# Neighbourhood attention with a mixture of experts: the combination's third array held in SBUF

## The reference

```python
x = x + _L0_conv_ref(_ln_c(x), ...)        # 7x7 neighbourhood attention, 16 heads, projection
t = _to_tokens(x)                          # 25088 tokens of 128 channels
t = t + _L0_ffn_ref(_ln_t(t), ...)         # experts
x = _from_tokens(t, x)

# _L0_ffn_ref: two of eight experts for each token
combine = (one_hot(topk_i, E) * topk_p[..., None]).sum(axis=1)
for e in range(E):
    h = relu(x_flat @ W1[e] + b1[e])
    out = out + combine[:, e:e + 1] * (h @ W2[e] + b2[e])
```

## Time and profile before

| | us |
|---|---|
| median of 3 runs | 3022.98 |
| lowest and highest | 3019.34, 3025.69 |
| the profiled execution | 3022.68 |
| its span, first to last instruction | 3020.9 |
| start of the second block (SP's first issue) | 2264.74 |
| first product of the experts | 2270.64 |
| last scatter issued by POOL | 2860.12 |
| first add of the combination, L1350 | 2868.77 |
| last add of the combination | 3017.23 |

### The profile page before, as it was taken

How to read it: one execution, slowest core, us unless ns; L and a number is a source line. 1 busy time by engine, 2 the same in 40 slices (tenths; PEclk the granted TensorE clock), 3 DMA queues, 4 the chain that set the end, 5 groups by cost and what they waited for, 6 DMA issues and landing times. The chain is left out here.

```text
span 3020.9 us, 112796 instructions
## 1 busy us (share of the span) xinstructions
PE 2688.8 (89%) x31346; PEld 2395.9 (79%) x31451; DVE 2269.4 (75%) x12559; ACT 2114.3 (70%) x5724; POOL 1583.9 (52%) x2025
## 2 busy tenths in 40 slices
PE   4789999999999999999999999999939999999733
PEld 2789999899989998999899989999936766776522
DVE  2668888788878887888788868888857888888655
ACT  1567878787878886887787868888847777777500
POOL 2135555455545554555455545555565777777600
PEclk9999999999999999999999999999969999999855
DMA  2665666555546664656566645566645444444399
GB/s 48 153 122 124 129 124 123 112 122 127 126 102 130 124 124 102 130 128 124 101 127 128 129 99 124 125 125 129 132 91 105 97 94 97 97 94 97 101 323 322
DMA packets 714047, 378.50 MB, mean 125 GB/s; under 512 B 422528, under 2 KB 669984, under 8 KB 713504
## 3 DMA queue, kind: packets, MB, share of 16 engines
q1 hardware_dynamic: 660704, 235.97, 40.3%
q10 hardware_dynamic: 24192, 81.67, 9.5%
q0 software_dynamic: 28608, 54.48, 6.1%
HBM read 233.43 MB, written 98.11 MB: 110 GB/s over the span
## 5 line engine op out<-in xcount | busy, mean ns | idle before, releaser
L1061 ACT ACTIVATE pr<-sc,nmx 128x100 f32<-128x100 f32 x3136 | 923.9, 369 | 61.9 <-DVE nmx L678 60.9
L962 POOL TENSOR_TENSOR oml<-om 128x256 f16<-128x256 f32 x784 | 479.6, 612 | 907.3 <-DVE om L708 890.4
L533 PE MATMUL bank<-vwin,pt 100*128 100x65 f32 x6272 | 806.2, 272 | 36.3 <-DVE om L708 28.1
L678 DVE CUSTOM_DVE_ANT_0 sc<-bank,near 128x100 f32<-128x100 f32 x3136 | 633.5, 257 | 253.7 <-PE bank L511 207.8
L533 PEld LDWEIGHTS bank<-vwin,pt 100*128 100x128 f32 x6272 | 773.4, 194 | 54.3 <-ACT pt L1069 39.5
L511 PE MATMUL bank<-kimg,held 128*128 (+2 forms) x9408 | 628.2, 216 | 40.9 <-issue 22.9
L511 PEld LDWEIGHTS bank<-kimg,held 128*128 128x128 bf16 (+1 forms) x9408 | 561.3, 100 | 88.3 <-issue 56.7
L1069 ACT ACTIVATE pt<-bank 100x512 f32<-100x512 f32 x784 | 460.6, 587 | 223.5 <-PE bank L520 208.8
L1367 POOL DMA_INDIRECT yrows<-ye,meta x420 | 449.2, 1070 | 154.6 <-issue 109.8
L930 POOL DMA_INDIRECT xrows<-rows,idx x448 | 433.9, 969 | 114.9 <-issue 75.5
L520 PE MATMUL bank<-cst_sb,pr 128*100 128x128 f32 x3136 | 477.1, 275 | 0.0
(11 more groups left out here) (133 smaller groups left out, 3366.8 us busy)
## 6 DMA issues: line engine op xcount, KB each, us to landing
vwin<-v_pix SPq DMA_DIRECT2D x1120, 60.5 KB
near<-bias_rows ACTq DMA_DIRECT2D x112, 600.0 KB, 4.7
y<-yrows SPq DMA_DIRECT2D x112, 224.0 KB, 4.3
held<-qring SPq DMA_DIRECT2D x896, 14.0 KB
v_pix<-vrow SPq DMA_DIRECT2D x56, 225.8 KB
xin<-in_x SPq DMA_DIRECT2D x56, 224.0 KB
xres<-in_x SPq DMA_DIRECT2D x112, 112.0 KB
x<-xres SPq DMA_DIRECT2D x112, 112.0 KB
```

The source lines that it names most:

```text
L533: mm = pe.matmul(ps_av[m % 2][:, 2 * t + blk, :], pt[:, m % 2, 2 * t + blk, :], vwin[:, st, 2 * u + t, 64 * blk:64 * blk + 65], start=True ...
L678: i = v.tensor_tensor_reduce(out=sc[:, ring(m, par), k, :], in0=ps_s[m % 2][:, k, :], in1=near[:, st, ct, k, :], scale=-1.0, scalar=-MASKE ...
L962: g.tensor_tensor(oml[:, st, u], om[:, st, u], om_h[:, st, u], ALU.subtract).then_inc(s["oml_done"], 1)
L1061: i = a.activation(pr[:, r, k, :], sc[:, r, k, :], ACT.Exp, bias=nmx[:, r, k:k + 1], scale=-1.0)
```

## The change

The combination no longer loads x1 chunk by chunk. ACT loads all of x1 into SBUF at the head of the second block, in nine transfers (L1381): 34 chunks into a larger xo, 13 into the columns of held behind the weights, 9 into stage1. The first add waits for all nine (z_home). To make room, y0 and y1 take the place of hf, which is free after the experts. The loop over chunks is written out, since the home of a chunk is chosen while the program is built. Of y0 and y1, the semaphore steps of a chunk go from 48 to 32.

```diff
--- before.py
+++ after.py
@@ -1174,16 +1174,24 @@
         hl = sb("hl", [128, HRING, T], BF16)
         ye = sb("ye", [128, XR, 4, C])
 
-        y0 = sb("y0", [HALF, ZR, QT, C])
-        y1 = sb("y1", [HALF, ZR, QT, C])
+        y0, y1 = (hf[0:HALF, k * ZR:(k + 1) * ZR, :].rearrange("p r (n c) -> p r n c", c=C) for k in range(2))
         ys = sb("ys", [HALF, 2, QT, C])
-        xo = sb("xo", [C, ZR, TOK])
+        rest_a, rest_b = held[:, 2 * E * FF:], stage1[:]
+        in_a, in_b = (4 * NTILE * HEADS * NQ - 2 * E * FF) // TOK, E * FF // TOK
+        xo = sb("xo", [C, (CT - in_a - in_b) * TOK])
+        homes = ((xo[:], CT - in_a - in_b), (rest_a, in_a), (rest_b, in_b))
+
+        def x1_chunk(c):
+            for home, room in homes:
+                if c < room:
+                    return home[:, c * TOK:(c + 1) * TOK]
+                c -= room
         oo = sb("oo", [C, 2, TOK])
 
 
         c_names = """b2_in m_yb w_small
             m_x0 m_x1 m_x2 m_x3 m_meta0 m_meta1 m_meta2 m_meta3 m_meta4 m_meta5 m_meta6 m_meta7 m_hpre m_hf m_hh m_hl m_y m_ye m_sc0 m_sc1 m_sc2 m_sc3
-            z_x0 z_x1 z_x2 z_x3 z_sum z_t z_out z_store0 z_store1""".split()
+            z_home z_x0 z_x1 z_x2 z_x3 z_sum z_t z_out z_store0 z_store1""".split()
         for n in c_names:
             s[n] = sem(n)
 
@@ -1200,12 +1208,10 @@
             assert NT % MR == 1
 
             def out_tiles(eng, body):
-                for c in range(ZR):
-                    body(c, c)
-                with eng.Fori(ZR, CT - ZR + 1, ZR) as c:
-                    for r in range(ZR):
-                        body(c + r, r)
+                for c in range(CT):
+                    body(c, c % ZR)
             assert CT % ZR == 0
+            PARTS = sum(-(-room // 7) for _, room in homes)
 
             @block.sync
             def _(sp):
@@ -1228,8 +1234,6 @@
                         .then_inc(s[f"m_meta{r}"], 16)
                 moe_tiles(sp, moe)
 
-                for r in range(ZR):
-                    sp.dma_start(xo[:, r, :], x1[:, r * TOK:(r + 1) * TOK]).then_inc(s[f"z_x{r}"], 16)
                 for r in range(XR):
                     sp.wait_ge(s[f"m_sc{r}"], 16 * 4 * ((NT - r + XR - 1) // XR))
 
@@ -1239,8 +1243,6 @@
                     for j, dst in ((0, y0), (1, y1)):
                         src = bass.AP(yrows.tensor, c * (TOK * C) + j * (NTOK * C), [[QT * C, HALF], [1, QT * C]])
                         sp.dma_start(dst[:, r].rearrange("p n c -> p (n c)"), src).then_inc(s[f"z_x{r}"], 16)
-                    if not early(c, ZR):
-                        sp.dma_start(xo[:, r, :], x1[:, bass.ds(c * TOK, TOK)]).then_inc(s[f"z_x{r}"], 16)
                 out_tiles(sp, fetch)
                 for par in range(2):
                     sp.wait_ge(s[f"z_store{par}"], 16 * (CT // 2))
@@ -1337,7 +1339,7 @@
                 gated(NT - 1, 0, last)
 
                 def add_rows(c, r):
-                    v.wait_ge(s[f"z_x{r}"], 48 * (c // ZR) + 48)
+                    v.wait_ge(s[f"z_x{r}"], 32 * (c // ZR) + 32)
                     if not early(c, 2):
                         v.wait_ge(s["z_t"], c - 1)
                     v.tensor_tensor(ys[:, r % 2], y0[:, r], y1[:, r], ALU.add).then_inc(s["z_sum"], 1)
@@ -1345,11 +1347,13 @@
                 def add_x1(c, r):
                     par = r % 2
                     v.wait_ge(s["z_t"], c + 1)
+                    if c == 0:
+                        v.wait_ge(s["z_home"], 16 * PARTS)
                     if not early(c, 2):
                         v.wait_ge(s[f"z_store{par}"], 16 * (c // 2))
                     v.tensor_tensor(oo[:, par].rearrange("c (p n) -> c n p", n=QT),
                                     bank[6 + par][:, 0:TOK].rearrange("c (n p) -> c n p", n=QT),
-                                    xo[:, r].rearrange("c (p n) -> c n p", n=QT), ALU.add).then_inc(s["z_out"], 1)
+                                    x1_chunk(c).rearrange("c (p n) -> c n p", n=QT), ALU.add).then_inc(s["z_out"], 1)
 
                 def combine(c, r):
                     add_rows(c, r)
@@ -1370,6 +1374,12 @@
 
             @block.scalar
             def _(a):
+                at_ = 0
+                for home, room in homes:
+                    for k in range(0, room, 7):
+                        n = min(7, room - k)
+                        a.dma_start(home[:, k * TOK:(k + n) * TOK], x1[:, at_ * TOK:(at_ + n) * TOK]).then_inc(s["z_home"], 16)
+                        at_ += n
                 a.wait_ge(s["w_small"], 16)
                 ps_h = bank[0:4]
                 a.wait_ge(s["t_ready"], 3)
```

## The result

| | us |
|---|---|
| after, median of 8 runs (lowest, highest) | 3049.37 (3044.76, 3058.05) |
| before, median of 8 runs beside them | 3034.35 (3019.34, 3038.62) |
| ratio of the means, 95% interval | 1.0064 (1.0042 to 1.0086) |
| the profiled execution of after, its span | 3044.76, 3042.8 |

The change makes the kernel slower by 0.6%, some 19 us by the means (3050.3 against 3030.9; the medians lie 15 us apart); 2995 was forecast, and the range ended at 3018. So stages are compared from that issue on. The times of SP's issue, the products and the scatters are those of the trace's first or last instruction of the line.

A forecast was written before the change was run, and what follows sets the result against it. The prediction took full DMA engines and the two-store ring as one bound on the combination, 2.70 us a chunk. Its sum: 3022.7 - 33.0 (combination) + 4 (experts' head) + 1 (written-out loop) = 2994.7, say 2995 us; range 2982 to 3018.

The forecast's parts named there:

- What bounds the kernel: Combination: full DMA engines and the ring of two stores, landing 4.1 us, are two readings of one 2.70 us pace.
- The store's landing, 2.76 us: Combination: landing falls from 4.1 to 2.76 us, a store-ring step of 2.02; 2.10 taken, 33.0 us less in all.
- with some queue left over from the chunk before, more: Combination: clause that leftover queue would raise the store-ring step above 2.02 us; no size given.
- the one with a step of 2.39: Rival, combination: landing falls only half way, to 3.5 us; 17 us less, 5 more, 3011; chance 0.12.
- the one in which the ring holds: Rival, combination: landing stays 4.1 us whatever the number of reads, step 2.70, kernel slower at 3028; chance 0.07.
- the prediction's own sum: Combination: store-ring step as add and issue, 1.28 us, plus landing, over two; (1.28 + 2.76) / 2 = 2.02 us.
- The head of the experts, 4 us: Start of the experts: x1's nine loads share engine time about evenly with SP's transposes; 4 us more, ends 0 and 31.
- The upper bound, 31 us: Start of the experts: all of the burst goes first, first transpose done at about 2301.4 instead of 2270.6.
- the experts starve: Rival, experts: long rows go one for each transposed row; 31 us more, 33 less, 1 more: 3022; chance 0.11.
- Only the first is late: Experts: later transposes need 3.3 us of engine time, under the tile's 5.5, so only the first transpose is late.
- The written-out loop, 1 us more: Combination: SP's saved address instructions gain nothing as it waits for DVE; straight code costs 0 to 3 us, 1 taken.
- Buffers in other places, z_home: nothing: Moved buffers keep instruction shapes, and the first add's wait for x1 is over 540 us early; no cost.

The follow-up runs named there:

- e7: The kernel before with four buffers for the combination's result instead of two, nothing else; 3030.30 us, ratio to before 0.9989.
- e11: The kernel before with four result buffers and the y fetch released by the sum of its rows, x1's fetch still by the result; 3025.40 us, ratio 0.9974.
- e2_short_rows: The kernel after with the same x1 bytes loaded at the head in six transfers of every second chunk, rows of 1792 B; 3039.72 us.
- e5_one_each: The kernel after with its nine head loads replaced by one chunk of x1 per tile, from tile 8 on; 3020.50 us, ratio to before 0.9962.
- e9_one_each_four_sum: The kernel of e5_one_each with four result buffers and the y fetch released by the sum of its rows; 2976.83 us, ratio to before 0.9817.
- e1_spread: The kernel after with its nine long loads issued one behind each of tiles 0 to 7, two behind tile 7; 3060.25 us, ratio to before 1.0111.

## Why the prediction was wrong, by its own steps

*What bounds the kernel.* It held two readings of the 2.70 us, full engines and the ring of stores, to be one. The transfers were the bound (e7, e11). But it did not follow that the ring would give way with them.

*The store's landing, 2.76 us.* This size was wrong, and with it the step (2.10 taken, 2.48 measured). It was made of a landing alone, 1.90, and one y row between each two rows of the store, 0.86. In the trace's packet records of after (medians over 48 stores) the interleaving is about as supposed: 151 y packets go between the 128 of a store. Two things were left out. The store's first packet starts 1.71 us after the issue, where a store alone takes 0.85; some 160 y packets start in that time, so I read it as standing behind y packets already queued. And a y packet takes 120 ns in the mean, not 107. So 1.90 + 0.86 ahead of the first packet + 151 / 128 x 8 x 0.120 = 1.13 between them is 3.9 us, the figure measured. The text's clause "with some queue left over from the chunk before, more" named the missing part and gave it no price. Of the rivals the one with a step of 2.39 was nearest; the one in which the ring holds was right in its mechanism, "the price of a store among reads whatever their number", and off in the size by 0.2 us of landing. With 3.9 us of landing the prediction's own sum gives (1.28 + 3.9) / 2 = 2.59; that 2.48 came out, nearer to 2.39, is luck, since address instructions went that the sum had left in.

*The head of the experts, 4 us.* This step failed by its mechanism. It took the earlier trace rows, 655 small packets to 132 long, to show that queues share time about evenly. At the head of the experts turns went row for row, 780 to 780. Why they did not in the stretch of the earlier trace rows is open: by the packet records some long rows start in every half microsecond of it, so the long queue had work; but the records do not tell the engines apart. The short rows there are plain ones of 516 B, and plain short rows beside plain long ones were not run; that plain rows as such go otherwise than a transpose's is not borne out, since those of 1792 B in e2_short_rows took turns with a transpose's one for one. A row of one pair of transfers was carried over to another pair. The upper bound, 31 us, was right to 0.6 us, and the rival "the experts starve" was this mechanism; it had a chance of 0.11 for no better reason than the earlier trace rows. The Trainium skill, DMA: Bandwidth & Descriptors, section "Queues, rings and completion order", has an engine take turns between the queue rows that it has work for by whole packets, typically of some 9 to 17 descriptors; the 780 to 780 of after, 256 B against up to 12,544 B at a time, do not bear that out for a transpose beside long rows, and the measurement decides. "Only the first is late" held in after, since the burst ended with the first transpose.

*The written-out loop, 1 us more.* This term had the wrong sign: it took SP's issues for the place where address instructions would be saved, and SP waits anyway, but ACT's stood in the ring of stores, an estimated 8.5 us. Against them stands a cost of about the size taken. Two steps of after are much longer than the others, from 2947.25 (4.17 us) and from 3028.18 (3.63 us), and in each a transfer of 16 KB on the instruction queue q8 starts, at 2948.1 and 3028.0 by the packet records; before's DMA view of 2875 to 3012 has no instruction queue. DVE waits in them for a store, as its timeline shows:

```profile
2951.42 0.94 DVE L1354 TENSOR_TENSOR oo<-bank,xo 128x448 f32<-128x448 f32 x1 [2.64 <-DMA out<-oo]
```

The two steps are 2.8 us over the mean. e5_one_each has two such steps, 3.92 and 3.55 us, beside such transfers; that they are the cause was not tested.

*Buffers in other places, z_home: nothing.* Right: PE and DVE have no wait for x1.

The sum with the measured sizes, from SP's first issue: + 30.4 + 0.5 - 12.2 = 18.7 us, against the 19 of the means (0.0064 x 3031).

## What to carry to other kernels

A bulk load of long rows beside a stream of transposes took turns with it row for row and stopped it: handed out in portions, with some of the stream's work in hand, it cost 2 to 4 us instead of 30. Cutting the load into short rows can hold the engine that issues it (29.7 us in e2_short_rows), and what that engine has to do behind it is late. A ring of two stores whose landing time equals the pace of full engines looks like their bound and is none, until bytes are taken away; take away bytes and deepen the rings together, since either alone may show little. How two queues share the engines is read from a stretch with the same two kinds of transfer, or left as wide as its bounds.

## What was not expected of the hardware

- A packet of 2048 B of y took 102 ns in before at 342 GB/s, 120 in after at 275 GB/s, and 86 in e9_one_each_four_sum at 396 GB/s (means of the packet records). The median is 84 ns in all three: what differs is a tail of slow packets, in after 877 of 11,274 over 200 ns, in e9 18 of 10,305. What the slow ones wait for is open.
- Four streams, two of them of x1 and the output, moved 334 to 343 GB/s at landings of 4.1 to 6.2 us; three moved 396 in e9, with DVE busy 35.80 of 40 us, so these may have room yet. What makes the fourth lower the rate is open too.
- Long rows of 12,544 B between transposed ones moved 426 GB/s at the head of after, and 135 GB/s in e1_spread, with engines partly free.
